# Cross-attention and feed-forward kernel on one core: who issues the first two key gathers, and where one query product stands in the prologue

## What is computed

```python
q = split_heads(layernorm(x) @ Wq.T + bq)      # 16 heads of 8
k = split_heads(ctx @ Wk.T + bk)
v = split_heads(ctx @ Wv.T + bv)
score = einsum('bhij,bhkj->bhik', k, q) / sqrt(8)
attn = softmax(score, axis=1)                  # over the 16 heads
x = x + (einsum('bhik,bhij->bhjk', attn, v) rearranged) @ Wo.T + bo
h = layernorm(x)
for blk in range(3):                           # 6 linear layers: dequantised weight + low-rank part
    y = gelu(layernorm(linear(h, 2*blk)) * gamma + beta)
    h = linear(y, 2*blk + 1) + h
out = x + h
```

## Time and profile before

| | |
|---|---|
| time, median of 3 runs | 362.67 us (361.74 to 363.77) |
| the profiled execution's own time | 362.27 us |
| its span in the profile | 360.4 us |
| PE busy | 340.1 us, 94% of the span |
| DVE busy | 331.7 us, 92% |
| ACT busy | 288.2 us, 80% |
| POOL busy | 266.8 us, 74% |

### The profile page before, as it was taken

One profiled execution on the slowest core, in us unless ns is written; L12 is line 12 of the kernel. 1 busy time (PEld: TensorE's weight loads), 2 busy tenths in 40 slices (PEclk: granted clock), 3 DMA queues, 4 the chain that ended last, 5 costly groups with the idle time before them and its releaser, 6 DMA issues.

```text
span 360.4 us, 13093 instructions
## 1 busy us (share of the span) xinstructions
PE 340.1 (94%) x4804; PEld 254.6 (71%) x4804; DVE 331.7 (92%) x821; ACT 288.2 (80%) x585; POOL 266.8 (74%) x288
## 2 busy tenths in 40 slices
PE   7888799999999999999999798988999999999995
PEld 6555367677667667766766566865888888888874
DVE  6899999999999999999999999979999999988774
ACT  4698588788788878878887767668889999999983
POOL 6609488878877977987897999878877788774231
PEclk9999899999999999999999999999999999999999
DMA  7879286467548547745834400000010000210112
GB/s 197 237 238 274 70 255 188 143 202 218 169 137 262 177 136 210 212 154 159 262 132 136 148 4 2 2 1 3 17 45 29 29 29 29 61 32 29 36 54 88
DMA packets 54531, 43.29 MB, mean 120 GB/s; under 512 B 4625, under 2 KB 48609, under 8 KB 54497
## 3 DMA queue, kind: packets, MB, share of 16 engines
q1 hardware_dynamic: 53920, 42.31, 38.8%
q10 hardware_dynamic: 576, 0.53, 0.5%
HBM read 26.05 MB, written 16.78 MB: 119 GB/s over the span
## 4 chain that ended last, share of the span: by engine, by line
PE 62%; DVE 23%; POOL 5%; issue 5%; ACT 3%; DVEq 0%; POOLq 0%; ACTq 0%
PE score_ps L1637 9%; PE att_ps L1600 7%; DVE zsum L847 6%; PE score_ps L1541 5%; DVE negmax L829 5%; PE wo_ps L1379 5%; PE score_ps L1391 3%; PE score_ps L1730 3%; PE work L1723 3%; PE work L1415 3%; POOL probs L524 3%; PE att_ps L1730 3%; PE score_ps L1631 2%; PE work L1428 2%; PE work L1421 2%
## 5 line engine op out<-in xcount | busy, mean ns | idle before, releaser
L524 POOL TENSOR_TENSOR probs<-probs,rz 128x1024 f32<-128x1024 f32 x64 | 136.2, 2141 | 37.0 <-DVE rz L850 36.9
L571 POOL TENSOR_TENSOR rs<-ve,minus_half 128x4 f32<-128x4 f32 (+1 forms) x47 | 55.6, 1184 | 34.3 <-DVE ve L778 24.7
L1139 ACT ACTIVATE probs<-score_ps 128x1024 f32<-128x1024 f32 x64 | 65.6, 1024 | 17.8 <-PE score_ps L1541 17.1
L847 DVE TENSOR_REDUCE zsum<-probs 128x64 f32<-128x1024 f32 x64 | 77.3, 1208 | 1.7 <-ACT probs L1139 1.5
L829 DVE TENSOR_REDUCE negmax<-score_ps 128x64 bf16<-128x1024 f32 x64 | 75.2, 1177 | 0.0
L1379 PEld LDWEIGHTS wo_ps<-wo_t,att_t 128*128 128x128 f32 x256 | 36.9, 191 | 13.4 <-issue 12.0
L1600 PE MATMUL att_ps<-probs,v_diag 128*32 128x64 f32 x2048 | 43.8, 225 | 2.1 <-POOL probs L524 2.1
L1637 PEld LDWEIGHTS score_ps<-lin_t,h 128*128 128x128 f32 x304 | 36.9, 191 | 11.1 <-DVE h L930 7.0
L1221 ACT ACTIVATE z<-score_ps,rs 128x128 f32<-128x128 f32 x152 | 43.5, 382 | 0.6 <-POOL rs L571 0.6
L1541 PE MATMUL score_ps<-negmax,ident_bf 128*128 128x512 bf16 x128 | 39.0, 386 | 4.7 <-DVE negmax L829 4.7
L1600 PEld LDWEIGHTS att_ps<-probs,v_diag 128*32 128x32 f32 x2048 | 33.2, 109 | 12.6 <-POOL probs L524 3.4
(11 more groups left out here) (263 smaller groups left out, 692.6 us busy)
## 6 DMA issues: line engine op xcount, KB each, us to landing
q_parts<-parts SPq DMA_DIRECT2D x15, 512.0 KB, 3.5
k_stack<-k_parts SPq DMA_DIRECT2D x30, 256.0 KB, 3.3
q_stack<-q_parts SPq DMA_DIRECT2D x60, 128.0 KB, 3.0
x_all<-in_x SPq DMA_DIRECT2D x16, 256.0 KB, 3.9
ctx_sb<-in_ctx SPq DMA_DIRECT2D x16, 256.0 KB, 3.7
k_parts<-parts SPq DMA_DIRECT2D x16, 256.0 KB, 2.9
out<-x_all SPq DMA_DIRECT2D x15, 256.0 KB, 2.3
q_parts<-parts SPq DMA_DIRECT2D x4, 128.0 KB, 2.4
```

The source lines that it names most:

```text
L524: nc.gpsimd.tensor_tensor(e[:, :, :, :], e[:, :, :, :], by_query.broadcast_to([P, BANDS, SEQ, ADJ]), ALU.mult).then_inc(s_probs, 1)
L571: nc.gpsimd.tensor_tensor(rs2[v][:, lo:hi], ve2[v][:, lo:hi], minus_half[:, lo:hi], ALU.pow).then_inc(p_rs[v], 1)
L847: nc.vector.tensor_reduce(zsum[q][:, :], probs[(p - 1) % 4][:, :, :, :].rearrange("p u k s -> p k u s"), AX_XY, ALU.add).then_inc(s_zsum, 1)
L1139: nc.scalar.activation(probs[p][:, :, :, :], score_ps[p % 2][:, :].rearrange("p (u s k) -> p u k s", s=ADJ, k=SEQ), ACT.Exp, scale=SCALE). ...
```

## The change

Two edits, both in the prologue. The two DMAs of `gather_first_k`, with their wait for the stored keys (`s_k_out`), leave ACT's queue, where they stood between `context_columns(1, 1)` and `input_columns(1)`, and enter SP's, between the first four gathers of q and the last four. On PE the product `project_q(1)` moves ahead of `low_rank_products(0)`. What is computed and what is moved stay the same.

```diff
@@ block.sync
+            def gather_first_k():
+
+                sp.wait_ge(s_k_out, 16)
+                src = k_dram[0].rearrange("(g r) l t -> (r l) g t", g=GROUPS)
+                for a in range(2):
+                    sp.dma_start(k_stack[0][a:P:2, :, :], src).then_inc(h_k_stack, 16)
...
                 gather_first_q(0, h_stack)
+                gather_first_k()
                 gather_first_q(1, s_stack[0])
@@ block.scalar
-            def gather_first_k():
-
-                act.wait_ge(s_k_out, 16)
-                src = k_dram[0].rearrange("(g r) l t -> (r l) g t", g=GROUPS)
-                for a in range(2):
-                    act.dma_start(k_stack[0][a:P:2, :, :], src).then_inc(h_k_stack, 16)
...
                 context_columns(1, 1)
-                gather_first_k()
                 input_columns(1)
@@ block.tensor
                 project_k(1, 1)
+                project_q(1)
                 low_rank_products(0)
-                project_q(1)
                 k_remainder(1, 1)
```

## The result

The changed kernel takes 363.36 us (median of 20 runs, 362.22 to 365.24), the kernel before beside it 362.21 us (20 runs, 361.47 to 363.77). The ratio is 1.0033, 95% interval 1.0019 to 1.0047: slower by 1.2 us, by 0.7 to 1.7 us within the interval. The time lies in the forecast range of 361.7 to 364.3, the sign is the forecast's, and the loss is about twice the +0.6 us of the sum. Each ratio in this document goes, with its interval, by the fast runs alone; it is not the quotient of the two medians beside it and can differ from that by 0.1%.

A forecast was written before the change was run, and what follows sets the result against it. A chain of DVE without gaps, then PE without gaps, bounds the kernel; 0 (ACT) + 0 (PE order) + 0.6 (negmax) + 0 to 0.1 (input load) gives 362.9 or 363.3 us by footing; forecast 363.1, range 361.7 to 364.3.

The forecast's parts named there:

- the sum: Whole kernel: ACT 0, PE order 0, first negmax +0.6 us, input load 0 to 0.1, together +0.6 us.
- Gate: First scores: start some 0.15 us behind the later of key and q gathers; PE is free only shortly before.
- Slack: Behind the first scores: they can slip 0 to 0.15 us for nothing and gain nothing by coming earlier.
- ACT: ACT's prologue queue: without two DMA issues xln_t starts about 1 us earlier, worth 0 at the first scores.
- PE order: PE prologue: query product and low-rank products swap; same work ends at the same time, near 19.2 us, worth 0.
- Landing of the keys: SP's key gathers: second issued 16.8 us, landing 19.95 us, negmax +0.6 us; bounds 0 and +1.25 us.
- The input load: SP's x_all load: issued 19.6 us, lands 3.1 us later, covered by the late negmax; 0 to 0.1 us.
- Chunk 1's stores and gathers: SP's queue, later: store of k from 19.41 to 20.05 us, its gathers following by about 0.6 us.
- Passing on: From first negmax to the end: DVE, then PE, without gaps, so a gain or loss arrives nearly whole.
- The clock rival: Low-clock stretch at 39.20 to 42.61 us goes away, chain gains 0.7 us: 362.2 or 362.6 us; chance 0.18.
- Nothing moves: Rival at the gathers: nearly full DMA engines land the last transfer when before; 362.4 to 363.0 us; chance 0.27.
- The slow rival: PE's idling before the first scores brings a second low-clock stretch, up to 1.7 us more: 365.0 us; chance 0.10.

The follow-up runs named there:

- e3: Kernel before, with only a wait added: the first scores also wait for the second half of the queries; 363.42 us against 362.40 (1.0041).
- e2: Kernel before, with only the query product moved ahead of the low-rank products on PE, ACT keeping the key gathers; 362.81 us against 362.40 (1.0014).
- e9: Changed kernel, with SP issuing the second half of q only once the keys have landed; 367.18 us once, run for the landings.
- e4: Changed kernel, with the two key gathers issued behind the first two q gathers instead of all four; 363.05 us against 362.40 before (1.0021).
- e5: Changed kernel, with key gathers behind the first two q gathers and the x_all load ahead of q's second half; 363.12 us against 362.36 before (1.0025).
- e7: Changed kernel, with five unneeded identity matmuls on PE ahead of the wait for the keys; 363.34 us against 362.36 before (1.0024).
- e6: Kernel before, unchanged, for a second profile; its prologue ran 4 us late from its start; 369.38 us.
- e11: Kernel before, unchanged, for another profile; 363.16 us, span 361.3 us.
- e1: Changed kernel with PE's old order, so only the key gathers move to SP; 363.33 us against 362.40 before (1.0020).
- e10: Changed kernel, unchanged, for a second profile; span 361.0 us at full clock.

## Why the prediction came out as it did

**Gate: right. Slack: slightly mis-sized.** The first scores waited for data and PE was free just before; e3 shows that their lateness alone gives the loss. I allowed up to 0.15 us of slack behind them and took 0.1 off the sum. There was none: scores and `negmax` both moved by 0.98 us.

**ACT: right.** `xln_t` came 1.1 us earlier, the query product with it, and nothing at the first scores used it.

**PE order: right, for the stated reason.** The remainder moved by 0.16 us, of which 0.07 is this execution's earlier start (the key product L1421 at 14.76 for 14.83 us). `w_eff`, which needs PE's last low-rank products, moved by the same 0.15 us. e2 shows the other half of that step: without edit one the same order costs PE 0.6 us.

**Landing of the keys: mechanism right, term mis-sized.** The second key gather was issued at 16.57 us, 0.2 earlier than forecast. I took 3.1 to 3.2 us from issue to landing, from SP's gather of chunk 1, and +0.6 us at `negmax`. It took 3.8 us (3.6, 3.8 and 4.1 in three more profiles), and `negmax` came 1.0 us later. The row I leaned on was the same form in the same queue, but at another time and beside other transfers. Holding back the second half of q in e9 took 0.5 us off; e4 and e5, at 3.3 and 3.2 us with gathers behind the keys, show that this isn't the whole cause, which stays open. I had the 3.7 us of ACT's contended gather as the upper bound, and that was the nearer row.

**The input load: right in kind.** It was issued at 19.32 us and landed after 3.5 (forecast 19.6 and 3.1). It was covered in the changed kernel (no wait on `x_all` at 23.12 us) and came out in e4 with 0.35 us. In e7's profile, with the same DMA order, it took 4.6 us to land and cost 0.69 us on top of the late scores, so the cover is thin and part of the changed kernel's slower runs may come from here.

**Chunk 1's stores and gathers: wrong in a part that didn't count.** I had them 0.6 us later. The store of k is 0.4 us later (19.80), the first key gather 0.46 us earlier (23.52 for 23.98).

**Passing on: right.** One for one, within the scatter of the table above.

**The sum.** At full clock +0.6 to +0.9 us by the medians, and +1.0 us by the trace: the medians are over executions in which the landings vary (3.6 to 4.1 us for the slower key gather in the changed order, 3.7 to 4.9 us in the order of before, in the profiles of before, e2, e3, e6 and e11), the trace compares two of them. The rest of the measured +1.2 us goes by the counts with the different share of low-clock runs, which is not shown to come from the change. That the forecast time of 363.1 us lies within 0.3 us of the measured 363.36 is in part luck: it stands on the median of three runs of before, 362.67 us, and the 20 runs gave 362.21. From there +0.6 us would be 362.8.

**The clock rival.** I read the disappearance of the low-clock stretch as something that the shift of PE's pause could do, at -0.7 us. In the changed kernel's profile it was indeed gone, and its price was near the forecast, 0.5 us by the runs and 0.7 by the table. But e11 shows the kernel before, without any shift, with one stretch more: their number changes from execution to execution. "Nothing moves" fell with the first profile. The slow rival was half right: a second place for a fall exists (20 us in e5 and e9), but neither profile of the changed kernel has it.

I argued that the clock wouldn't fall because it didn't after 2.25 us of PE work in 3.42 us. That argument was wrong: in e5 it fell after 2.42 us in 3.42, in e9 after 2.75 in 3.41, and in the changed kernel it held after 2.13:

```profile
18.72:22.13 3.41, 2.13 (x43) 1.69 (x43) 2.06 (x4) 2.19 (x7) 0.00 (x0) 1.00 0.78 230
```

The busy time of a stretch in this view doesn't decide it by itself.

The Trainium skill's rule that issuing from a second engine saves only the issuing time ("DMA: Bandwidth & Descriptors", "Issuing engines are not separate DMA queues") was the argument for a smaller loss. The runs agree with its first half, that transfers interleave whoever issued them: the fourth q gather on SP's queue took 3.8 us with ACT's key gathers in flight and 2.0 us without. They agree with the limit too: the keys were issued 1.25 us later (16.57 for 15.3) and the scores came 0.98 us later. What failed was my reading of it as a sum of 0 to 0.6 us. The same section of the Trainium skill calls the saved issuing time usually small beside the DMA itself; here it was 1.25 us beside a landing of 3.8, and it was on the path.

## What to carry to other kernels

Where a wait needs two sets of data, look at when both land: moving one behind the other in a single queue brings one early for nothing and the other late at full price. Take a transfer's landing time from a row with the same traffic around it, not only from one of the same shape, and give it the spread that several profiles show. And compare spans only at equal granted clock, run by run, before reading a few tenths of a per cent.

## What the runs showed of the hardware

Transfers of two queues slowed each other: the slowest of the four 64 KB q gathers took 3.8 us to land beside ACT's 256 KB key gathers (3.7 in e3 and e11, 3.5 in e2) and at most 2.3 us without them (the changed kernel, e1, e7, e9, e10). Within one queue the last key gather landed after 3.3 us with nothing issued behind it (e9), but also after 3.3 and 3.2 us with gathers behind it (e4, e5), and after 3.6 to 4.1 us in the order of the changed kernel. The slower key gather of one program, the kernel before, took 3.7, 3.9 and 4.9 us in three executions. The low-clock stretches were 3.4 us or twice that, in the profiles between 39 and 49 us and between 207 and 219 us in kernels of both kinds, in e5 and e9 also from 20 us and in e9 from 30 to 37 us, and their number differed between executions of one program. One such stretch went with 0.5 us of median span (360.5 for 360.0), two with 1.4 us (361.4 in 14 executions of before with a mean clock of 0.989 to 0.991).
